# A two-layer graph kernel on one core: x loads moved, items halved, evacuations reordered at two items

## The reference

```python
def _gcn_layer(x, adj, W, b):
    d_inv_sqrt = (jnp.sum(adj, axis=1) + 1e-09) ** (-0.5)
    msg = d_inv_sqrt[:, None] * adj * d_inv_sqrt[None, :] @ x
    return jax.nn.relu(msg @ W + b)
H_f = _gcn_layer(feature_x, adj, W_f, b_f)
H_s = _gcn_layer(spatial_x, adj, W_s, b_s)
attn = jax.nn.sigmoid(jnp.concatenate([H_f, H_s], axis=1) @ W_att + b_att)
return _layernorm(x + attn * H_f + (1.0 - attn) * H_s)
```

## Time and profile before

| | |
|---|---|
| median of three runs (lowest, highest) | 392.65 us (392.62, 392.72) |
| the profiled execution | 393.04 us |
| its span, from first to last instruction | 391.2 us |
| mean granted TensorE clock | 0.994 |
| busy PE, DVE, ACT, POOL | 378.3, 303.2, 285.6, 155.3 us |
| moved by DMA | 130.77 MB, mean 334 GB/s |

### The profile page before, as it was taken

One profiled execution on the slowest core, in us unless ns is written; L12 is line 12 of the kernel. 1 busy time (PEld: TensorE's weight loads), 2 busy tenths in 40 slices (PEclk: granted clock), 3 DMA queues, 4 the chain that ended last, 5 costly groups with the idle time before them and its releaser, 6 DMA issues. The chain is left out here.

```text
span 391.2 us, 5501 instructions
## 1 busy us (share of the span) xinstructions
PE 378.3 (97%) x1778; PEld 314.0 (80%) x1778; DVE 303.2 (77%) x443; ACT 285.6 (73%) x381; POOL 155.3 (40%) x204
## 2 busy tenths in 40 slices
PE   7889999999999999999999999999999999999992
PEld 7667778788888888788888888888788888888992
DVE  2789997999578975769578583928976796889795
ACT  3668788888877887878878887778742666687556
POOL 2332611571066402670058220010100417877795
PEclk9999999999999999999999999999999999999997
DMA  8999999999999999999999999999775534445002
GB/s 268 423 417 424 420 412 421 423 419 418 421 416 421 423 418 420 421 420 422 418 423 420 424 414 423 413 390 415 232 281 208 213 108 160 164 157 168 4 25 81
DMA packets 24556, 130.77 MB, mean 334 GB/s; under 512 B 2640, under 2 KB 7632, under 8 KB 10448
## 3 DMA queue, kind: packets, MB, share of 16 engines
q1 hardware_dynamic: 24528, 130.43, 83.2%
HBM read 128.32 MB, written 2.10 MB: 333 GB/s over the span
## 5 line engine op out<-in xcount | busy, mean ns | idle before, releaser
L533 DVE TENSOR_TENSOR Al<-raw,Ah 128x2048 fp32r<-128x2048 f32 (+2 forms) x101 | 162.0, 1620 | 40.3 <-ACT Ah L721 40.2
L408 PE MATMUL sums<-Ah,Yh 128*128 128x512 f32 (+1 forms) x484 | 186.9, 386 | 1.3 <-DVE Al L533 1.3
L409 PE MATMUL sums<-Ah,Yl 128*128 128x512 f32 (+1 forms) x484 | 185.1, 382 | 0.0
L410 PE MATMUL sums<-Al,Yh 128*128 128x512 f32 (+1 forms) x484 | 185.0, 382 | 0.0
L721 ACT ACTIVATE Ah<-raw 128x2048 fp32r<-128x2048 f32 (+2 forms) x101 | 127.1, 1283 | 48.9 <-DMA raw<-in_At 29.9
L731 ACT ACTIVATE nat<-nat 128x2048 f32<-128x2048 f32 (+1 forms) x54 | 100.1, 1855 | 20.0 <-DMA nat<-in_adj 19.3
L408 PEld LDWEIGHTS sums<-Ah,Yh 128*128 128x128 f32 x484 | 91.0, 188 | 22.5 <-DVE Al L533 4.8
L410 PEld LDWEIGHTS sums<-Al,Yh 128*128 128x128 f32 x484 | 91.0, 188 | 17.9
L409 PEld LDWEIGHTS sums<-Ah,Yl 128*128 128x128 f32 x484 | 91.0, 188 | 17.1
L553 DVE TENSOR_TENSOR acc<-sums,acc 128x512 f32<-128x512 f32 (+1 forms) x122 | 76.8, 673 | 28.8 <-PE sums L410 25.2
L871 POOL TENSOR_TENSOR S<-S,raw 128x512 f32<-128x512 f32 x40 | 62.4, 1559 | 32.2 <-DMA raw<-in_At 29.2
(11 more groups left out here) (56 smaller groups left out, 201.2 us busy)
## 6 DMA issues: line engine op xcount, KB each, us to landing
raw<-in_At SPq DMA_DIRECT2D x63, 1024.0 KB, 9.8
nat<-in_adj SPq DMA_DIRECT2D x47, 1024.0 KB, 12.0
nat<-in_adj SPq DMA_DIRECT2D x8, 768.0 KB, 9.6
xs<-in_xs SPq DMA_DIRECT2D x5, 512.0 KB, 11.1
out<-xs SPq DMA_DIRECT2D x15, 128.0 KB, 1.8
xs<-in_xs SPq DMA_DIRECT2D x5, 256.0 KB, 11.5
nat<-in_adj SPq DMA_DIRECT2D x2, 512.0 KB, 6.6
raw<-in_At SPq DMA_DIRECT2D x2, 512.0 KB, 8.5
```

Source lines behind the costliest of these rows:

```text
L408: pe.matmul(to, Yh[:, t % YRING, hs], high, start=first, stop=False)
L409: pe.matmul(to, Yl[:, t % YRING, hs], high, start=False, stop=False)
L410: mm = pe.matmul(to, Yh[:, t % YRING, hs], low, start=False, stop=last)
L533: dve.tensor_tensor(Al[:, k % SPLITS, a * IB:b * IB], raw[:, k % RAWS, a * IB:b * IB], Ah[:, k % SPLITS, a * IB:b * IB], ALU.subtract).the ...
```

## The change

`HALVED` becomes two numbers. `BY_BLOCK` = 22 keeps all that concerns the order of PE and the rules of evacuation; `IN_PARTS` = 50 says up to where items are made in two pieces, so items 22 to 49 now are, with `first_block` on PE. x of four tiles is loaded behind `raw` of the item before the one that needs it (items 22, 29, 37, 46, 48) instead of four before (19, 26, 34, 43, 45). At items 47 and 48 DVE's order is written anew, and the fourth run that ends in item 45 (`LATE`) is evacuated behind the runs that end in item 47.

```diff
-HALVED = 22
+BY_BLOCK = 22
+IN_PARTS = 50
...
-    evac_order = sorted(range(len(runs)), key=lambda e: done_no[e, 0])
+    LATE = next(e for e in range(len(runs)) if end_item[e] == FINAL - 3 and runs[e][2] == 3)
+    evac_order = sorted(set(range(len(runs))) - {LATE}, key=lambda e: done_no[e, 0])
+    evac_order.insert(1 + max(evac_order.index(e) for e in evac_order if end_item[e] == FINAL - 1), LATE)
...
-    X_AFTER = {y_position(m * GT) - 4: m for m in range(3, G)}
+    X_AFTER = {y_position(m * GT) - 1: m for m in range(3, G)}
...
-            return [(0, 2), (2, GT)] if k < HALVED else [(0, GT)]
+            return [(0, 2), (2, GT)] if k < IN_PARTS else [(0, GT)]
...
-                    in_first = k < HALVED and j == 0
+                    in_first = k < IN_PARTS and j == 0
...
                 for a, b in pieces(k):
                     low(k, a, b)
                     if a == 0:
-                        if k >= HALVED and len(ending) == GT:
+                        if k >= BY_BLOCK and len(ending) == GT:
                             evacuate_new(ending[:2])
-                        if k in (FINAL - 1, FINAL):
-                            evacuate_new(ending[:1])
-                        for r in y_at[k]:
+                        if k == FINAL:
+                            evacuate_new(ended)
+                        if k != FINAL - 1:
+                            for r in y_at[k]:
+                                y_low(r)
+                    elif k == FINAL - 1:
+                        evacuate_new(ending[:1])
+                        for r in y_at[k][:2]:
+                            y_low(r)
+                    elif k == FINAL:
+                        for r in y_at[k - 1][2:]:
                             y_low(r)
...
-                if k < HALVED or k in (FINAL - 1, FINAL):
+                if k < BY_BLOCK:
                     evacuate_new(ending)
+                if k == FINAL:
+                    evacuate_new(ending + [LATE])
...
                 if k < K - 1:
-                    evacuate_new(ended)
+                    evacuate_new([e for e in ended if e != LATE])
```

More of the change, by code:

```diff
@@ L95, in sweeps @@
             n = i
-            while k >= HALVED and n < len(items[k]) and items[k][n][0] == items[k][i][0]:
+            while k >= BY_BLOCK and n < len(items[k]) and items[k][n][0] == items[k][i][0]:
                 n += 1
@@ L648, in _ @@
                 ending = [e for e in evac_order if end_item[e] == k - 1]
-                if k < HALVED:
+                if k < BY_BLOCK:
                     evacuate_new(ending[:2])
@@ L658, in _ @@
                     if a == 0:
-                        if k >= HALVED and len(ending) == GT:
+                        if k >= BY_BLOCK and len(ending) == GT:
                             evacuate_new(ending[:2])
-                        if k in (FINAL - 1, FINAL):
-                            evacuate_new(ending[:1])
-                        for r in y_at[k]:
+                        if k == FINAL:
[9 more added lines that the diff above has]
+                        for r in y_at[k - 1][2:]:
                             y_low(r)
                     third_now = a == (1 if k < STEPWISE else 0) and items[k][0][0] != items[k][1][0]
-                    if k < HALVED and third_now:
+                    if k < BY_BLOCK and third_now:
                         evacuate_new(ending[:3])
-                if k < HALVED or k in (FINAL - 1, FINAL):
+                if k < BY_BLOCK:
                     evacuate_new(ending)
+                if k == FINAL:
+                    evacuate_new(ending + [LATE])
                 if k == COLLECT + 2:
```

## The result

| kernel | median of the runs (lowest, highest) | ratio to before, 95% interval |
|---|---|---|
| before | 392.64 us (392.49, 393.13), 22 runs | 1 |
| changed | 393.63 us (391.97, 395.40), 22 runs | 1.0029, 1.0018 to 1.0041 |

The change makes the kernel slower by 1.0 us, 0.3%, and its runs spread over 3.4 us where those of before keep within 0.64. They form groups: two of 22 lie at 392.0 and 392.25, fourteen at 393.1 to 393.7, six at 394.6 to 395.4. The profiled execution took 393.41 (span 391.6), one of the middle group.

What follows compares the result with a forecast made beforehand. PE was taken to bound items 22 to 50, losing 1.25 us there. 0.94 + 0.31 − 0.05 (half of the reserve) = 1.2 us less, so the median 392.65 would be 391.45; range 391.2 to 392.5.

Steps and rivals of the forecast that it cites:

- 0.94 at items 26 to 29: PE loses 0.70, 0.17 and 0.07 us around items 26 to 29 from a late raw load; all gained.
- 0.31 at item 48: PE loses 0.19 and 0.12 us at items 47 and 48 to DVE; the new order removes this.
- 0.5 spare: Item 49: second half of Al done at 23.3, wanted at 23.8; nothing lost, with 0.1 as reserve.
- rival 1: The stall at 48 moves to item 49, losing 0.6 to 0.8 us; time 392.1; chance 16%.
- So either part alone removes the stall: Item 27: first half of Al comes 2.4 us early with both parts, 1.8 early without the x part.
- Item 42 also takes longer, by the 16 column-sum matmuls behind it, which stay.: Item 42 on PE: its extra time was set aside as unchanged and not counted in the 1.25 us.
- 0.36 for the first block: Item 45's first block: both column halves worked together, so the first evacuation pair ends at 2.53 instead of 2.17.
- in its waits for Ah or PE: DVE hides the halves' extra work, 0.07 us per item by starts, in these waits, except at items 46 to 49.
- The other four loads move likewise.: The other x loads also go three items later; raw 47 and 48 have 1.25 us less load ahead.
- rival 2: The stall at 27 is passed on to items 30 or 31; gain 0.4 us, time 392.25; chance 7%.
- rival 3: The change does not reach PE because the stalls are one execution's jitter; gain 0 to 0.5 us; chance 7%.
- rival 4: Loads starve as SP issues raw k + 3 only after all of Al k; 1.35 us slower, 394.0; chance 7%.

Runs made afterwards that it cites:

- run 5: The kernel before with only the x load of m = 4 moved, from behind raw 26 to behind raw 29; 391.71 us, ratio 0.9975.
- run 6: Changed kernel with halves for items 46 to 49 only and, of the x loads, only m = 4 moved; 391.89 us, ratio 0.9981.
- run 8: Changed kernel, fourth pair of item 41 evacuated before Al of item 43, x load of m = 3 back behind raw 19; 391.49 us, ratio 0.9976.
- run 12: The changed kernel measured again, nothing else changed; 395.04 us, ratio 1.0054.
- run 1: Changed kernel with the fourth pair of item 41 evacuated before Al of item 43 instead of behind it; 393.31 us, ratio 1.0014.
- run 3: Changed kernel with the x loads at their old places, so halves and new order only; 393.66 us, ratio 1.0024.
- run 4: The kernel before with one added DVE addition in front of the fourth evacuation of item 41; 393.54 us, ratio 1.0034.
- run 9: Changed kernel with only the x load of m = 3 back behind raw 19; 393.32 us, ratio 1.0011.
- run 2: The kernel before with only the x loads moved three items later; 392.51 us, ratio 0.9988.
- run 10: Changed kernel, x load of m = 3 back, two added matmuls filling PE's wait before the column sums; 391.66 us, ratio 0.9977.

## Why the prediction was wrong

- **0.94 at items 26 to 29: right**, in the changed profile and by run 5 alone (0.91 between the medians).
- **0.31 at item 48: right in the profile, but not kept.** Item 49, where the prediction left 0.5 spare, loses 0.4 to 0.5 in the profiles of runs 6, 8 and 12 and 1.77 in that of run 1. In all four DVE waits for Ah of item 48 (0.66 to 0.72, in run 1 1.32, which puts Al 48 at 278.42), where the changed kernel's first profile has no such wait (276.53), and Al 49 slips behind it: rival 1's mechanism, at half to two and a half times its price. It adds to the spread and does not decide the median.
- **"So either part alone removes the stall": wrong for the halves.** The x load alone does it (run 5), the halves alone leave 0.50 at item 27 (run 3). The sum for 27 took only the first half of Al and left out the evacuation behind the second. It cost the forecast nothing, since both parts were in.
- **The step that failed first: "Item 42 also takes longer, by the 16 column-sum matmuls behind it, which stay."** They stay (they are eight matmuls, seen as 16 records), but they wait for a pair that DVE evacuates in item 43, with 0.24 to spare in the kernel before. The prediction had both terms that used it up, 0.36 for the first block and 0.07 for each split item, and charged them only at items 46 to 49; for the rest it said that DVE hides them "in its waits for Ah or PE". A wait of DVE hides its work only from those who do not wait for that work. The wait itself costs 0.5, and the half clock behind it some 1.6 in many runs (three of eight in run 4, four of six in run 12, and by their times eight of eleven in run 9). No rival had it.
- **The step that failed second: "The other four loads move likewise."** Their effect on raw 47 and 48 was followed, that of m = 3 was costed at nothing. Raw 20 lands earlier, which helps nobody, and starts GpSimd's sums beside DVE's Yl and Al of item 19, and stretches them by 1.05 and 1.11. PE wants that Al 12 matmuls into the item, at 120.20 + 2.72 = 122.92 in the kernel before, where it was done at 121.46: 1.46 of spare against 2.16. That costs 0.85 at item 19 in the larger part of the runs (by their times seven of eleven in run 2), and the two profiles of the halved kernel that have it (runs 1 and 12) lose another 0.7 to 0.8 in item 35. The kernel before already had such a row: the first half of Al 19 takes 2.21 beside a sum, not 1.21.
- **Rivals 2, 3 and 4: not seen.** Nothing is passed on to items 30 and 31; the DMA rate falls by 1% only. The forecast of a slower kernel rested on starving loads; the slower kernel came from DVE's order.
- **The number.** Without the two failed steps the change is what was forecast: run 8 gains 1.13 for the forecast 1.2 and has 391.49 for the predicted 391.45; that they meet within 0.04 is in part luck, as its profile loses 0.42 in item 49 that the forecast did not have. The range was too narrow because it held only stalls at the places that the change was read for.

## What to carry to other kernels

When an edit makes an engine's chain longer in total and shorter to its first piece, list everyone who waits for the chain's last instruction, one-off consumers too, with the spare that each has in the trace: here a spare of 0.24 us, used up, cost up to 2.1. An earlier load is not free either; ask which engine it starts, and what that runs beside. And where a kernel's runs fall into groups, one profile shows one group: take away one suspected cause at a time and see which group disappears.

## What the runs showed of the hardware

**TensorE's clock.** PE at full clock, then 0.4 to 0.5 us of waiting, then the column sums, 16 records of one column each that begin 0.11 us apart, together 1.8 us up to the next wide matmul: after that the granted clock is the lower level for 3.4 us in some executions and not in others. Of the five profiles with this wait one shows it. With the wait filled by two matmuls of 128 columns, or absent, no profile shows it and no execution has a mean clock below 0.988; 0.984 to 0.986 occur only in the changed kernel and in runs 3, 4 and 12, which all have the wait. A mean of 0.989 proves nothing: six of the fourteen profiles have another such stretch from about 13 us on, shortly behind a wait of PE's (1.78 us, up to 11.95, in the changed kernel's first profile; granted clock 0.83 from 10 to 20 us there, 1.00 in that of before). What tells one execution from the next was not found, nor how short a wait is harmless; neither was tried.

**DVE beside GpSimd.** An instruction of DVE with two SBUF inputs grows by 1.0 to 1.1 us when it begins soon after GpSimd began to add two SBUF tiles (0.47 to 1.52, 1.21 to 2.31), and by less when the sum is nearly through: a Yl of run 8 begun 0.87 into a sum (200.97 against 200.10) takes 0.71. Evacuations, with one input in PSUM, do not grow: a pair takes 1.27 beside a sum (209.74 in run 12, the sum from 209.29) and 1.28 without one. The Trainium skill (SBUF — State Buffer, section "Who interferes with whom") says that a DVE instruction with two inputs in SBUF contends with a GpSimd instruction that reads SBUF, for read ports that the two engines share and that are locked exclusively. The trace agrees: in run 2 the sum that begins at 120.73 ends at 122.02, and 1.21 later, at 123.23, the Al would be done if it waited for all of it; it is done at 123.11.

**What stands open.** The stalls of item 49 (0 to 1.8 us) were not taken apart, nor that of item 35, and what Ah of item 48 waited for was not followed. Runs 5, 8 and 10 all beat the kernel before, by 0.9 to 1.1 us; their intervals overlap, so none of them is shown to be the best. Run 5 is one edited line.
